# Graph network with mixture of experts: one packed word per visit for TensorE's block numbers, and another order of its waits

## The chip, the cores and the metric

The kernel runs on 1 core of one Trainium2 chip. The metric is the device time of one execution in microseconds (us); what is given is the median of several runs. Before the change it is 3036.38 us, the median of 3 runs.

## What is computed

x has 3125 nodes of 768 features; src and dst name 50000 edges, sorted by dst. Three graph attention layers with 12, 12 and 1 heads stand in a residual branch, then a mixture of 8 experts with 2 chosen per token stands in a second one:

```python
def _gat_layer(x, W, attn_l, attn_r, bias, src, dst, num_heads, head_dim, use_elu):
    z = (x @ W).reshape(N, num_heads, head_dim)
    el = jnp.sum(z * attn_l, axis=-1)
    er = jnp.sum(z * attn_r, axis=-1)
    e = jax.nn.leaky_relu(el[src] + er[dst], NEG_SLOPE)
    m = jax.ops.segment_max(e, dst, num_segments=N)
    ex = jnp.exp(e - m[dst])
    denom = jax.ops.segment_sum(ex, dst, num_segments=N)
    alpha = ex / denom[dst]
    msg = alpha[:, :, None] * z[src]
    out = jax.ops.segment_sum(msg, dst, num_segments=N)
    out = out + z + bias.reshape(1, num_heads, head_dim)
    if use_elu:
        out = jax.nn.elu(out)
...
x = x + _L0_gnn_ref(_layernorm(x), ...)          # three layers, use_elu in the first two
x = x + _L0_ffn_ref(_layernorm(x)[None], ...)[0] # softmax of the top 2 router logits, 8 experts, 192 wide, exact gelu
```

The change touches only how TensorE finds its way in the sums over the edges (`out` and `denom`) and in the term `er[dst]`.

## The kernel before

Nodes lie in NB = 25 blocks of 128, edges in ET = 391 tiles of 128. As the edges are sorted by dst, a tile meets one block or a few; a pair of tile and block that meet is a **visit**, and there are V = ET + NB - 1 = 415. b(k), the block of visit k, depends on the edges, so the kernel works it out on the chip at the start. VectorE's prologue (L1254 to L1263) writes it in several layouts: `b_k`; `b_of` (L1260, L1261), five numbers for each of NG = 83 groups of G = 5 visits, which TensorE reads; `b_g` (L1257 to L1259), the first block of a group and of the next, which ScalarE reads; `ends`, the last visit of each block. `turns` (written at L1756) is read by GpSimd in the expert part (L641).

Each layer has a node sweep (z = x @ W, stored to a table in HBM) and then an **edge sweep** over the 415 visits. NBUF = 4 groups are one trip of a loop, U = 20 visits; 20 trips are rolled, the 21st (3 groups) is written out. For a visit:

- GpSimd gathers 128 rows of z by src into a slot of 20 (L672). It waits for s_agg, the count of visits that TensorE has added up, so that the slot is free.
- VectorE builds ST_b, the one-hot matrix of a group from the edge's place in the block (L1445).
- TensorE multiplies ST_b with `erp`, the er values of block b in three bf16 parts: three small matmuls at L1022 (`er_of_edges`), whose address comes from b. The last one of a group raises s_er.
- VectorE forms the exponents (L1475, L1480; L1457 to L1469 in the third layer), ScalarE takes exp (L821, L822) and builds the one-hot S (L830, L834).
- VectorE weighs the rows: L1492 in the first two layers (raises s_msg), S_weighted at L1498 and S at L1494 in the third. Five or six visits of a trip (SPLIT) go another way: ScalarE copies a leading part (L781, L784, L785), VectorE the rest (L1509; L1512, L1513), which raises s_rest.
- TensorE adds the visit to its block in PSUM (`add_up`, L1028 to L1049): four passes of 384 or so columns at L1047 into banks that are chosen by the parity of b, then s_agg rises.
- Once a block is complete, ScalarE copies its sums out and clears the banks (`close_blocks`, L788; L805, L810, L814), which raises s_acc_free. It reads `b_g` at L790.

Each engine runs its own instruction list, and they meet in semaphores only. On TensorE `body` (L1051) sets the order: for each group g it loads the five block numbers of g (`now`), adds up visit 0, loads the five of g + ER_LEAD = g + 3 (`later`), and puts the er matmuls of group g + 3 behind the visits 1 (two of them) and 3 (three). Ahead of the loop the er matmuls of the groups 0 to 2 are done. A load (`blocks_of`, L1010 to L1015) is one instruction that fills five registers of TensorE's sequencer from SBUF. What depends on b is then computed by the sequencer: the address of `erp` (L1022), the value of the wait on s_acc_free (L1042), the bank (L1047). In `add_up` the waits come in this order: s_rest (L1035) or s_msg (L1039), s_acc_free (L1042), and s_S at the first visit of a group in the first two layers (L1044).

Of the kernel before, what the change touches and what calls it, by code (L numbers as in the profile page):

```python
# [8 lines left out]
I32 = mybir.dt.int32  # L9
U32 = mybir.dt.uint32  # L10
U8 = mybir.dt.uint8
# [14 lines left out]
G = 5  # L26
NBUF = 4
IN_ARENA = 3
ER_LEAD = 3
U = G * NBUF  # L30
VISITS = ET + NB - 1
V = -(-VISITS // G) * G
# [67 lines left out]
def gnn_ffn(nc, x, edges, gnn, ffn, out):  # L100
    with ExitStack() as ctx:
# [64 lines left out]
        src_k = sb("src_k", [P, V], I32)  # L166
        dst_k = sb("dst_k", [P, V])
        b_k = sb("b_k", [1, V + 1], I32)
        b_g = sb("b_g", [1, NG, 4], I32)
        b_of = sb("b_of", [1, NG + ER_LEAD, 8], I32)  # L170
        ends = sb("ends", [1, NB], I32)
        turns = sb("turns", [1, NS], I32)
        erm = sb("erm", [P, NB, 2 * HMAX])
        ert = sb("ert", [P, NB, HMAX])
        erp = sb("erp", [P, NB * 3 * 2 * HMAX], BF16)
# [753 lines left out]
        def _(pe):  # L929
# [74 lines left out]
            def edge_sweep(l):  # L1004
                H = HEADS[l]

                for bank in range(4):
                    nc.tensor.matmul(PS[:, bank, :], zeros_h[:, 0:P], zeros_h[:, :], start=True, stop=True)

                def blocks_of(g):  # L1010

                    return nc.values_load_multi_w_load_instructions(
                        b_of[0:1, bass.ds(g, 1), 0:G].rearrange("o i j -> o (i j)"), engines=[mybir.EngineType.PE],
                        min_val=0, max_val=NB - 1,
                        skip_runtime_bounds_check_because="b(k) is a sum of NB - 1 comparisons")[1]  # L1015

                def er_of_edges(g, jj, j, b):

                    if j == 0:
                        pe.wait_ge(s_ST, g + (NG * l + 1))  # L1020
                    for part in range(3):
                        o = nc.tensor.matmul(er_of(l, jj)[:, j, :], ST_b[:, jj, j * P:(j + 1) * P],  # L1022
                                             erp[:, bass.ds(b * (6 * H) + part * 2 * H, 2 * H)],
                                             start=(part == 0), stop=(part == 2))
                    if j == G - 1:
                        o.then_inc(s_er, 1)

                def add_up(g, i, jj, j, b):  # L1028

                    at = jj * G + j  # L1030
                    odd = (b + l) % 2
                    flat = PS[:, :, :].rearrange("p b n -> p (b n)")
                    if at in SPLIT[l]:
                        n = SPLIT[l].index(at)
                        pe.wait_ge(s_rest, len(SPLIT[l]) * i + (n + 1 + split_before(l)))  # L1035
                        onehot = S[:, jj, j, :]
                        rows = [parts[:, n, part, :] for part in range(2)]
                    else:
                        pe.wait_ge(s_msg, g * G + (V * l + j + 1))  # L1039
                        onehot = f32(S[:, jj, j, :]) if H > 1 else S_weighted[:, jj, j, :]  # L1040
                        rows = [edge_row(l, at)]
                    pe.wait_ge(s_acc_free, b + (NB * l + 1))  # L1042
                    if H > 1 and j == 0:
                        pe.wait_ge(s_S, g + (NG * l + 1))  # L1044
                    for c, n in ((0, HALF), (1, sum_width(l) - HALF)):
                        for row in rows:
                            o = nc.tensor.matmul(flat[:, bass.ds(odd * 1024 + 512 * c, n)], onehot,  # L1047
                                                 row[:, c * HALF:c * HALF + n], start=False, stop=True, skip_group_check=True)
                    o.then_inc(s_agg, 1)  # L1049

                def body(i, last):  # L1051
                    groups = LAST_GROUPS if last else NBUF
                    for jj in range(groups):
                        g = NBUF * i + jj
                        ahead = not last or jj + ER_LEAD < groups
                        now = blocks_of(g)
                        for j in range(G):
                            add_up(g, i, jj, j, now[j])
                            if j == 0 and ahead:
                                later = blocks_of(g + ER_LEAD)  # L1060
                            if j in (1, 3) and ahead:
                                for n in ((0, 1), (2, 3, 4))[j // 2]:
                                    er_of_edges(g + ER_LEAD, (jj + ER_LEAD) % NBUF, n, later[n])

                pe.wait_ge(s_erm, l + 1)
                for g in range(ER_LEAD):
                    now = blocks_of(g)
                    for j in range(G):
                        er_of_edges(g, g, j, now[j])
                with pe.Fori(0, NI - 1) as i:  # L1070
                    body(i, False)
                body(NI - 1, True)
# [126 lines left out]
        def _(dve):  # L1199
# [58 lines left out]
            link(nc.vector.tensor_copy(b_g[0:1, :, 0:1], starts[:, :, 0:1]))  # L1258
            link(nc.vector.tensor_copy(b_g[0:1, 0:NG - 1, 1:2], starts[:, 1:NG, 0:1]))  # L1259
            link(nc.vector.memset(b_of[0:1, :, :], 0))  # L1260
            link(nc.vector.tensor_copy(b_of[0:1, 0:NG, 0:G], starts))  # L1261
            link(nc.vector.tensor_copy(ends[0:1, 0:NB - 1], enter[0:1, :]))
            link(nc.vector.memset(ends[0:1, NB - 1:NB], V))  # L1263
            augment_first((2, 3, 4))
# [595 lines left out]
```

## Time and profile before

| | |
|---|---|
| median of 3 runs | 3036.38 us (3032.83 to 3039.52) |
| span of the profiled execution | 3059.8 us |
| TensorE matmuls | 2691.3 us busy (88%), 14056 instructions |
| VectorE | 2096.8 us (69%), 3895 |
| ScalarE | 1244.9 us (41%), 2607 |
| GpSimd | 1506.0 us (49%), 1528 |
| HBM | 253 GB/s over the span |

The profiled execution's own time is read by its span; it lies 23.4 us over the median of the runs. Busy times of different engines overlap, so they don't add up to the span. "<- issue" names idle time of an engine in which it waited for nothing that the profile shows. The edge sweeps lie at 258 to 903, 1116 to 1762 and 1965 to 2610 us or so.

### The profile page before, as it was taken

What the parts mean: (1) busy time and instruction counts of PE and PEld (TensorE: products, weight loads), DVE (VectorE), ACT (ScalarE), POOL (GpSimd) and SP (SyncE); (2) the same over time, 40 slices, a digit from 0 to 9 for tenths busy, and PEclk for the clock granted to TensorE, in tenths of its full rate; (3) what the DMA queues carried; (4) which work ended last, traced back from release to release, by engine and by line L of the source; (5) the groups of instructions that cost most, each with busy time, mean ns of one, the idle gap of its engine ahead of it and who ended that gap; (6) DMA issues with size and microseconds to landing.
All of it is one profiled execution on the core that took longest, in us unless ns stands there. A gap on an engine that the chain in (4) does not pass through costs nothing.

```text
span 3059.8 us, 57119 instructions
## 1 busy us (share of the span) xinstructions
PE 2691.3 (88%) x14056; PEld 1838.6 (60%) x14060; DVE 2096.8 (69%) x3895; ACT 1244.9 (41%) x2607; POOL 1506.0 (49%) x1528
## 2 busy tenths in 40 slices
PE   3997999998989979898989999788898889759998
PEld 2884555555558855555555578555555555547776
DVE  6776888888887768888878877545555555673332
ACT  1224555555544435555555544223222223622211
POOL 1005666666631156666666412466666665114443
PEclk9998999999999979999999999899999999979999
DMA  6447888888867878888888767788888887967776
GB/s 210 169 148 251 289 286 291 291 290 290 289 219 205 210 228 292 289 287 290 291 287 288 250 191 216 218 281 285 279 282 281 282 282 258 397 217 145 145 146 118
DMA packets 199261, 762.09 MB, mean 249 GB/s; under 512 B 41889, under 2 KB 58033, under 8 KB 198542
## 3 DMA queue, kind: packets, MB, share of 16 engines
q0 software_dynamic: 127632, 604.14, 64.8%
q1 hardware_dynamic: 53790, 108.21, 11.6%
q10 hardware_dynamic: 17760, 48.79, 4.0%
q8 instruction: 36, 0.59, 0.1%
q14 instruction: 43, 0.35, 0.0%
HBM read 640.01 MB, written 133.45 MB: 253 GB/s over the span
## 4 chain that ended last, share of the span: by engine, by line
PE 50%; DVE 21%; issue 13%; ACT 4%; DMA 4%; another core or an unknown queue 3%; SPq 2%; POOL 1%; DVEq 1%; ACTq 1%; POOLq 0%
PE PS L1047 30%; DVE arena L1492 5%; PE PS L1176 5%; PE PS L978 4%; PE PS L1165 4%; PE PS L980 2%; DVE parts L1509 2%; PE PS L1022 2%; DMA arena<-table,src_k 2%; SPq L493 1%; DVE ST_b L1445 1%; DVE arena L1357 1%; DVE arena L1367 1%; DVE arena L1335 1%
## 5 line engine op out<-in xcount | busy, mean ns | idle before, releaser
L672 POOL DMA_INDIRECT arena<-table,src_k x945 | 959.9, 1016 | 500.8 <-issue 213.1
L1047 PE MATMUL PS<-arena,S 128*128 128x384 f32 (+1 forms) x1848 | 706.8, 514 | 57.8 <-issue 46.3
L1492 DVE TENSOR_TENSOR arena<-arena,PS 128x768 f32<-128x768 f32 x630 | 575.2, 946 | 0.9 <-ACT arena L822 0.9
L1047 PEld LDWEIGHTS PS<-arena,S 128*128 128x128 f32 x1848 | 335.5, 194 | 282.7 <-issue 156.8
L1047 PE MATMUL PS<-parts,S 128*128 128x384 f32 (+2 forms) x1332 | 340.4, 375 | 57.2 <-issue 51.0
L672 POOL DMA_INDIRECT W<-table,src_k x300 | 295.9, 986 | 160.5 <-PE PS L1047 71.2
L1047 PE MATMUL PS<-arena,S_weighted 128*128 128x384 f32 (+1 forms) x840 | 319.9, 516 | 33.4 <-issue 25.3
L1022 PEld LDWEIGHTS PS<-erp,ST_b 128*128 128x128 bf16 x3735 | 193.9, 97 | 249.9 <-issue 184.2
L618 POOL DMA_DIRECT2D table<-arena x75 | 41.6, 555 | 557.7 <-DVEq L1379 382.3
L1047 PEld LDWEIGHTS PS<-parts,S 128*128 128x128 f32 x1332 | 223.7, 192 | 106.0 <-issue 97.5
L830 ACT ACTIVATE apart<-iota_row,dst_k 128x128 f32<-128x128 f32 x830 | 261.7, 389 | 60.8 <-issue 44.1
L781 ACT ACTIVATE parts<-arena 128x780 fp32r<-128x780 f32 x168 | 142.0, 849 | 309.2 <-DVE arena L1492 136.7
L1022 PE MATMUL PS<-erp,ST_b 128*128 x3735 | 213.0, 172 | 54.0 <-issue 38.9
L1047 PE MATMUL PS<-W,S 128*128 128x396 f32 (+1 forms) x640 | 239.8, 502 | 14.6 <-issue 8.1
L1047 PEld LDWEIGHTS PS<-arena,S_weighted 128*128 128x128 f32 x840 | 154.3, 196 | 143.7 <-issue 79.4
L978 PE MATMUL PS<-W_lead,S 128*128 128x512 f32 x450 | 190.4, 423 | 9.8 <-DVE xT_rest L1383 7.9
L1509 DVE TENSOR_TENSOR parts<-arena,parts 128x780 fp32r<-128x780 f32 x168 | 162.0, 964 | 35.7 <-issue 24.4
L1492 DVE TENSOR_TENSOR W<-W,PS 128x768 f32<-128x768 f32 x200 | 182.4, 944 | 0.0
L978 PE MATMUL PS<-W_lead,xT_rest 128*128 128x512 f32 x450 | 179.2, 398 | 0.0
L978 PE MATMUL PS<-W_rest_r,S 128*128 128x512 f32 x450 | 178.7, 397 | 0.0
L1047 PEld LDWEIGHTS PS<-W,S 128*128 128x128 f32 x640 | 116.1, 190 | 91.3 <-issue 39.0
L1795 DVE TENSOR_SCALAR arena<-PS,gate_of 128x768 f32<-128x768 f32 x56 | 57.0, 1018 | 162.5 <-PE PS L1176 162.5
(293 smaller groups left out, 4354.1 us busy)
## 6 DMA issues: line engine op xcount, KB each, us to landing
arena<-mixed SPq DMA_DIRECT2D x63, 384.0 KB, 3.6
table<-arena POOLq DMA_DIRECT2D x50, 396.0 KB, 3.3
local_b<-local SPq DMA_DIRECT2D x123, 160.0 KB
mixed<-sums ACTq DMA_DIRECT2D x50, 384.0 KB
arena<-table SPq DMA_DIRECT2D x50, 384.0 KB, 4.6
arena<-table,src_k POOLq DMA_INDIRECT x945
table<-arena POOLq DMA_DIRECT2D x25, 384.5 KB, 4.6
out<-last_bias POOLq DMA_DIRECT2D x25, 384.0 KB, 6.4
```

Of the source, the lines that this page charges most:

```text
L672: nc.gpsimd.indirect_dma_start(edge_row(l, k % U)[:, 0:table_width(l)], None, table[l][:, :], bass.IndirectOffsetOnAxis(src_k[:, k:k + 1]. ...
L781: nc.scalar.activation(parts[:, n, 0, 0:D + H], row[:, 0:D + H], ACT.Copy).then_inc(s_leading, 1)
L830: o = nc.scalar.activation(apart[:, j, :], iota_row[:, :], ACT.Abs, scale=-1.0, bias=dst_k[:, bass.ds(g * G + j, 1)])
L978: nc.tensor.matmul(PS[:, 4 + 2 * b.q, :], rows[x_part], W_parts[W_part][:, 0:512], start=start, stop=stop)
L980: o = nc.tensor.matmul(PS[:, 5 + 2 * b.q, 0:z_width(l) - 512], rows[x_part], W_parts[W_part][:, 512:z_width(l)], start=start, stop=stop)
L1022: o = nc.tensor.matmul(er_of(l, jj)[:, j, :], ST_b[:, jj, j * P:(j + 1) * P], erp[:, bass.ds(b * (6 * H) + part * 2 * H, 2 * H)], start=(p ...
L1047: o = nc.tensor.matmul(flat[:, bass.ds(odd * 1024 + 512 * c, n)], onehot, row[:, c * HALF:c * HALF + n], start=False, stop=True, skip_grou ...
L1165: o = nc.tensor.matmul(to, token_xT(b.q)[:, k * P:(k + 1) * P], WiT[:, k, bass.ds(e * FF, FF)], start=(k == 0), stop=(k == KC - 1))
L1176: o = nc.tensor.matmul(PS[:, 4 + 2 * b.q + c, 0:HALF], hT(b.q)[0:rows, j * P:(j + 1) * P], flat[0:rows, bass.ds(e * (2 * D) + (2 * c + j) ...
L1492: nc.vector.tensor_tensor(z, z, a, ALU.mult).then_inc(s_msg, 1)
L1509: nc.vector.tensor_tensor(low[:, 0:D + H], row[:, 0:D + H], f32(high[:, 0:D + H]), ALU.subtract).then_inc(s_rest, 1)
L1795: nc.vector.tensor_scalar(zr(b.q, D).rearrange("p (c d) -> p c d", c=2), PS[:, 4 + 2 * b.q:6 + 2 * b.q, 0:HALF], gate_of[:, bass.ds(b.n, 1 ...
```

## The change

`b_of` keeps five words for each group, and a word now holds two numbers: b of the visit, plus 256 times b of the visit three groups ahead (for the last three groups only the former). VectorE adds the second part in the prologue with one scalar_tensor_tensor. TensorE loads the words of a group once, takes `word & 255` where it used `now` and `word >> 8` where it used `later`; the second load of a group is gone. In `add_up` the waits are reordered: s_acc_free, then s_S, then s_rest or s_msg. `b_g` and `turns` are held in bytes.

```diff
@@ -27,6 +27,7 @@
 NBUF = 4
 IN_ARENA = 3
 ER_LEAD = 3
+LOW = 256
 U = G * NBUF
 VISITS = ET + NB - 1
 V = -(-VISITS // G) * G
@@ -166,10 +167,10 @@
         src_k = sb("src_k", [P, V], I32)
         dst_k = sb("dst_k", [P, V])
         b_k = sb("b_k", [1, V + 1], I32)
-        b_g = sb("b_g", [1, NG, 4], I32)
-        b_of = sb("b_of", [1, NG + ER_LEAD, 8], I32)
+        b_g = sb("b_g", [1, NG, 4], U8)
+        b_of = sb("b_of", [1, NG, 8], I32)
         ends = sb("ends", [1, NB], I32)
-        turns = sb("turns", [1, NS], I32)
+        turns = sb("turns", [1, NS], U8)
         erm = sb("erm", [P, NB, 2 * HMAX])
         ert = sb("ert", [P, NB, HMAX])
         erp = sb("erp", [P, NB * 3 * 2 * HMAX], BF16)
@@ -1011,8 +1012,14 @@
 
                     return nc.values_load_multi_w_load_instructions(
                         b_of[0:1, bass.ds(g, 1), 0:G].rearrange("o i j -> o (i j)"), engines=[mybir.EngineType.PE],
-                        min_val=0, max_val=NB - 1,
+                        min_val=0, max_val=(NB - 1) * (LOW + 1),
                         skip_runtime_bounds_check_because="b(k) is a sum of NB - 1 comparisons")[1]
+
+                def now(word):
+                    return (word & (LOW - 1)).with_bounds(min_val=0, max_val=NB - 1)
+
+                def later(word):
+                    return (word >> 8).with_bounds(min_val=0, max_val=NB - 1)
 
                 def er_of_edges(g, jj, j, b):
 
@@ -1030,6 +1037,9 @@
                     at = jj * G + j
                     odd = (b + l) % 2
                     flat = PS[:, :, :].rearrange("p b n -> p (b n)")
+                    pe.wait_ge(s_acc_free, b + (NB * l + 1))
+                    if H > 1 and j == 0:
+                        pe.wait_ge(s_S, g + (NG * l + 1))
                     if at in SPLIT[l]:
                         n = SPLIT[l].index(at)
                         pe.wait_ge(s_rest, len(SPLIT[l]) * i + (n + 1 + split_before(l)))
@@ -1039,9 +1049,6 @@
                         pe.wait_ge(s_msg, g * G + (V * l + j + 1))
                         onehot = f32(S[:, jj, j, :]) if H > 1 else S_weighted[:, jj, j, :]
                         rows = [edge_row(l, at)]
-                    pe.wait_ge(s_acc_free, b + (NB * l + 1))
-                    if H > 1 and j == 0:
-                        pe.wait_ge(s_S, g + (NG * l + 1))
                     for c, n in ((0, HALF), (1, sum_width(l) - HALF)):
                         for row in rows:
                             o = nc.tensor.matmul(flat[:, bass.ds(odd * 1024 + 512 * c, n)], onehot,
@@ -1053,20 +1060,18 @@
                     for jj in range(groups):
                         g = NBUF * i + jj
                         ahead = not last or jj + ER_LEAD < groups
-                        now = blocks_of(g)
+                        words = blocks_of(g)
                         for j in range(G):
-                            add_up(g, i, jj, j, now[j])
-                            if j == 0 and ahead:
-                                later = blocks_of(g + ER_LEAD)
+                            add_up(g, i, jj, j, now(words[j]))
                             if j in (1, 3) and ahead:
                                 for n in ((0, 1), (2, 3, 4))[j // 2]:
-                                    er_of_edges(g + ER_LEAD, (jj + ER_LEAD) % NBUF, n, later[n])
+                                    er_of_edges(g + ER_LEAD, (jj + ER_LEAD) % NBUF, n, later(words[n]))
 
                 pe.wait_ge(s_erm, l + 1)
                 for g in range(ER_LEAD):
-                    now = blocks_of(g)
+                    words = blocks_of(g)
                     for j in range(G):
-                        er_of_edges(g, g, j, now[j])
+                        er_of_edges(g, g, j, now(words[j]))
                 with pe.Fori(0, NI - 1) as i:
                     body(i, False)
                 body(NI - 1, True)
@@ -1258,7 +1263,10 @@
             link(nc.vector.tensor_copy(b_g[0:1, :, 0:1], starts[:, :, 0:1]))
             link(nc.vector.tensor_copy(b_g[0:1, 0:NG - 1, 1:2], starts[:, 1:NG, 0:1]))
             link(nc.vector.memset(b_of[0:1, :, :], 0))
-            link(nc.vector.tensor_copy(b_of[0:1, 0:NG, 0:G], starts))
+            link(nc.vector.tensor_copy(b_of[0:1, :, 0:G], starts))
+            blocks = bk_f()[0:1, :].rearrange("o (g j) -> o g j", j=G)
+            link(nc.vector.scalar_tensor_tensor(out=b_of[0:1, 0:NG - ER_LEAD, 0:G], in0=blocks[:, ER_LEAD:, :], scalar=float(LOW),
+                                                in1=blocks[:, 0:NG - ER_LEAD, :], op0=ALU.mult, op1=ALU.add))
             link(nc.vector.tensor_copy(ends[0:1, 0:NB - 1], enter[0:1, :]))
             link(nc.vector.memset(ends[0:1, NB - 1:NB], V))
             augment_first((2, 3, 4))
```

## Rows read from the trace of the kernel before

**Rows 1.** the page: its span, and the chain that ended last, by line

```profile
span 3059.8 us, 57119 instructions
...
PE PS L1047 30%; DVE arena L1492 5%; PE PS L1176 5%; PE PS L978 4%; PE PS L1165 4%; PE PS L980 2%; DVE parts L1509 2%; PE PS L1022 2%; DMA arena<-table,src_k 2%; SPq L493 1%; DVE ST_b L1445 1%; DVE arena L1357 1%; DVE arena L1367 1%; DVE arena L1335 1%
```

**Rows 2.** three windows: us, PE, PEld, DVE, ACT, POOL busy, PEclk, DMA share, GB/s

```profile
261.00:902.00 641.00, 582.72 (x2860) 348.47 (x2860) 534.86 (x768) 348.11 (x827) 411.06 (x406) 0.98 0.87 285
1118.00:1760.00 642.00, 574.56 (x2860) 345.11 (x2860) 534.91 (x769) 348.81 (x828) 407.83 (x405) 0.98 0.86 284
1967.00:2608.00 641.00, 570.42 (x2860) 348.98 (x2860) 344.79 (x1079) 183.89 (x404) 403.23 (x405) 0.97 0.86 278
```

**Rows 3.** TensorE's waits, whole run: us in total, times, longest

```profile
PE PS L1047 <- issue: 136.5, 283, 5.0
PE PS L1022 <- issue: 38.9, 70, 1.3
PE PS L952 <- DVEq L1269: 19.1, 1, 19.1
...
PE PS L1047 <- DVE arena L1492: 15.0, 19, 3.2
...
PE PS L1047 <- DVE S_weighted L1498: 6.9, 6, 5.7
...
PE PS L1047 <- ACT PS L814: 0.4, 2, 0.2
```

**Rows 4.** TensorE's sequencer, four lines: ns min/median/max, first and last start

```profile
L1012 PEldq TENSOR_LOAD <-b_of x498: 5/582/1751, 249.9 to 2596.9; - x166
L1012 PEldq FUSED_REGOPS  x360: 4/60/726, 261.5 to 2582.9; - x180
...
L1022 PEldq FUSED_REGOPS  x3735: 2/46/728, 250.8 to 2588.8; - x197
...
L1047 PEldq FUSED_REGOPS  x2490: 2/51/1412, 261.2 to 2602.2; - x192
...
L1042 PEldq ALU_OP  x1245: 2/32/737, 260.9 to 2601.5; - x178
```

**Rows 5.** the same columns, within 829.0 to 831.5 us alone

```profile
L1022 PEldq FUSED_REGOPS  x9: 46/46/46, 829.1 to 830.1; - x9
...
L1039 PEldq ALU_OP  x1: 32/32/32, 830.2 to 830.2; - x1
...
L1042 PEldq ALU_OP  x1: 32/32/32, 830.3 to 830.3; - x1
...
L1047 PEldq FUSED_REGOPS  x2: 46/70/93, 830.4 to 830.6; - x2
...
L1012 PEldq TENSOR_LOAD <-b_of x1: 581/581/581, 830.8 to 830.8; - x1
...
L1039 PEldq FUSED_REGOPS  x1: 42/42/42, 831.5 to 831.5; - x1
```

**Rows 6.** TensorE's timeline, two places: start us, us, ... [idle before <-releaser]

```profile
742.49 1.48 PE L1047 MATMUL PS<-arena,S 128*128 128x384 f32 x4
743.81 0.38 PE L1022 MATMUL PS<-erp,ST_b 128*128 x9
...
822.22 1.57 PE L1047 MATMUL PS<-W,S 128*128 128x384 f32 x4 [0.17 <-issue]
...
826.07 1.57 PE L1047 MATMUL PS<-arena,S 128*128 128x384 f32 x4 [0.54 <-issue]
```

**Rows 7.** L1012 within 824.0 to 826.1 us

```profile
L1012 PEldq TENSOR_LOAD <-b_of x1: 1404/1404/1404, 824.2 to 824.2; - x1
```

**Rows 8.** GpSimd's waits in the first edge sweep, 258 to 903 us

```profile
POOL arena L672 <- PE PS L1047: 69.5, 70, 2.3
```

**Rows 9.** the tiles b_of and b_g

```profile
L1261 DVE COPY b_of<-b_k x1: 580/580/580, 25.5 to 25.5; 1x415 int32<-1x415 int32 x1
...
L790 ACTq TENSOR_LOAD <-b_g x249: 4/494/907, 272.9 to 2601.3; - x125
```

## The prediction

> **What bounds the kernel now.** Start with the page: L1047, the line where TensorE adds the messages up, is alone 30% of the chain that ended last, in a span of 3059.8 us [rows 1]. It runs in the three edge sweeps, and there the change works.
>
> Next, the sweeps by themselves [rows 2]. They are equally long, 641 to 642 us, with 2860 matmuls each, though VectorE works 535 us in the first two and 345 us in the third, and ScalarE 348, 349 and 184 us. So neither sets the length. TensorE, busy 570 to 583 us at a clock of 0.97 to 0.98, comes nearest; it is idle 58 + 67 + 71 = 196 us in the three together, and that is all that a change of TensorE's orders alone can win.
>
> Then what ended this idle time [rows 3]: 136.5 us before L1047 and 38.9 us before L1022 end with "issue", 175 us of the 196. Late messages (L1492) end 15.0 us in 19 waits, late S_weighted 6.9 us in 6, the accumulator (L814) 0.4 us in 2. So TensorE waits for its own sequencer much more than for data.
>
> The sequencer's own instructions [rows 4]: 498 loads of block numbers (median 582 ns), 360 fused register operations for their addresses, a fused one for each er matmul (3735), two for each add_up (2490), and a plain ALU_OP for each wait on the accumulator (1245). What one of them holds up is read from starts, not durations [rows 5]: nine fused ones of L1022 start within 829.1 to 830.1, 0.125 us apart, with the order of their matmul between them; the ALU_OPs of L1039 and L1042 start at 830.2 and 830.3 and the next instruction at 830.4, so 0.1 us each though the rows say 32 ns; the load starts at 830.8 and the next one at 831.5, 0.65 us. A visit of er_of_edges costs the sequencer 3 x 0.125 = 0.375 us.
>
> **The sequencer's bill.** Removed: the second load in each group of the loop, 80 groups x 3 layers = 240 loads x 0.65 = 156 us, and half of the 360 address operations, 180 x 0.1 = 18 us. Together -174 us.
>
> Added: a word is no longer a block number. Each add_up takes word & 255 (1245), as do the er visits ahead of the loop (15 x 3 = 45); each er visit in the loop takes word >> 8 (240 x 5 = 1200). Together 2490 operations of a kind that the trace of before doesn't show. Nearest row: a plain ALU_OP such as L1042's, 0.1 us of the queue, +249 us. From below: the operation goes into a fused instruction that is there already; the two at L1047 last 46 and 93 ns [rows 5], so one more piece inside costs 0.047 us, +117 us; lower still, nothing. From above: each of the three er matmuls computes its own address (3735 at L1022), and if the shift is evaluated anew each time there are 3600 in place of 1200, +240 us more. I take 0.1 us, once per visit, since L1042 shows an operation by itself as a plain instruction. The net is +249 - 174 = **+75 us** of sequencer time; the other ends are 117 - 174 = -57, -174, and 75 + 240 = +315.
>
> **How much of it reaches the array?** Four passes of an add_up take 1.32 us of the array (742.49 to the er matmuls at 743.81), the sequencer orders them in some 0.4 us (830.4 to 830.8, [rows 5]): there it gets ahead. Nine er matmuls take 0.38 us, and the sequencer needs 9 x 0.125 = 1.1 us for them: there it falls behind. Both show [rows 6]: 0.17 us of idle time at 822.22, and 0.54 us at 826.07, right after a load that held the sequencer from 824.2 for 1404 ns [rows 7]. The shifts stand in the er stretches, where the lead is used up, 5 x 0.1 us in a group; the ANDs stand at the add_ups, where cover is 1.3 us of passes; the removed load stood behind the first add_up of a group, under its passes. All of the +75 exposed is the upper end, none of it the lower. I take 0.4 of it, because half of what is added (the shifts) has poor cover and the rest good: **+30 us**. This is chosen between ends, not read.
>
> [...] The array went idle at 826.07 behind a load, though the passes before it had been ordered. [...]
>
> **The order of the waits.** add_up now waits for the accumulator, then S, then the message. While a message is late, the ALU_OP of L1042 (0.1 us), and its wait, are done beforehand instead of behind it. The late ones with a row are 19 + 6 [rows 3]; others arrive just ahead of their matmul and are hidden in "issue". At 0.1 us each it is -2.5 us for 25 and -12 for a tenth of the 1245 visits; nothing if passes cover it. I take **-8 us**. A cost where the accumulator is late: queued behind it are the message wait, which blocks nothing else on TensorE, and the next passes; it is late twice for 0.4 us in all [rows 3], so nothing, up to +1 us.
>
> **The small ones.** VectorE's prologue gets one operation over 400 words; the copy beside it takes 0.58 us [rows 9] and lies on the path, since TensorE waits 19.1 us at L952 for this prologue [rows 3]: +0.6 us, the smaller memset gives nothing to speak of. b_g and turns become bytes: the same number of loads, for b_g 249 of 494 ns on ScalarE [rows 9], and ScalarE isn't the bound; nothing, or 1 us either way. No DMA is added, removed or moved past another queue.
>
> **The sum.** +30 - 8 + 0.6 = +22.6 us on the profiled execution. Its span, 3059.8 us, is 23.4 us over the median of the runs, 3036.38; the difference is carried over: 3036.4 + 22 = **3058 us**.
>
> What is late next? GpSimd waits for a slot that an add_up frees 69.5 us in 70 waits of the first sweep [rows 8]: the gathers follow TensorE, so a slower TensorE delays them too and nothing makes it good; a faster one meets a DMA share of 0.86 to 0.87 [rows 2] before it gets 196 us back.
>
> **Rivals.**
> 1. *More of the bill is paid* (0.15). All of the +75 shows: 3036 + 75 - 8 = 3103; with the shift evaluated for each matmul 0.4 x 315 = 126, 3154. About 3090 is likeliest here. For it: a fused operation for each of three parts at L1022. Against: passes of 1.3 us over orders of 0.4 us.
> 2. *Faster* (0.30). Place: the load behind the first add_up of a group. One piece of 0.65 us, 1.4 us at times, empties the queue (0.54 us idle at 826.07), while scattered pieces of 0.1 us hide under passes. It decides once an operation holds the queue for less than 174 / 2490 = 0.07 us, or the load is exposed more than 249 / 174 = 1.4 times as much as the operations. With fused operations and an exposure of 0.4, 0.4 x -57 - 8 = -31: 3005. With half of the loads worth 0.3 us and no operation exposed, -36 - 8: 2992. For it: rows 6 and 7. Against: L1042, and that half of the operations stand where the lead is gone.
> 3. *No difference* (0.15). Orders hide under passes both ways, or the gathers set the pace (DMA share 0.87): 3028 to 3042.
> 4. *The change doesn't do what it says*: both loads remain in the code that is built. Then +249 of queue at 0.4 are +100, 3128. Its sign would be the 498 loads; I count it inside the 0.15 of rival 1.
>
> **How the numbers follow.** The forecast, partly exposed and slower, has 0.40 and holds 3043 to 3080. With rival 1 slower has 0.55; no difference 0.15; faster 0.30. The bound is 0.2%, 6 us, about what a measurement of this kernel can tell from no change. 2990 to 3100 takes in rival 2's reckoned times and most of rival 1, and leaves under 2 in 10 outside. As cases of both signs hold much of the chance, the likeliest one's own range of 3043 to 3080 is the one to compare.
>
> **What would show it.** L1012 keeps 258 loads and 180 fused ones. New ALU_OPs stand at the lines of now and later, some 2490; if instead the fused ones at L1047 and L1022 last longer, it is rival 2; with some 4900, rival 1. "Issue" before L1022 rises from 38.9 us by 20 or more, that before L1047 stays; waits on L1492 shrink; the three sweeps stay alike at 648 to 652 us. If they are shorter although the ALU_OPs are there, the exposure is what I had wrong.

## The result and the profile after

The changed kernel takes 3042.44 us (median of 20 runs, 3038.39 to 3049.03), the kernel before 3036.26 us (20 runs, 3030.68 to 3050.54): ratio 1.0022, with a 95% interval of 1.0014 to 1.003. It is 6.2 us slower. The forecast was 3058 us, 22 us slower.

The page of the changed kernel, its span and the chain by line:

```profile
span 3045.3 us, 58032 instructions
...
PE PS L1054 23%; DVE arena L1500 8%; PE PS L979 7%; PE PS L1181 5%; PE PS L981 4%; PE PS L1170 4%; DVE parts L1517 3%; DVE W L1500 2%; DMA arena<-table,src_k 2%; DVE ST_b L1453 2%; POOL arena L673 2%; SPq L494 2%; PE PS L1029 1%; PE PS L1154 1%
```

L1054 is the old L1047. The profiled execution is 14.5 us *shorter* than the one of before, though the medians say the reverse: single executions of either kernel differ by 10 to 20 us, so a difference of 6 us isn't read from two of them. What can be read is what kind of instruction stands where.

The changed kernel's own three sweeps, from the first er matmul to the last add_up, with the columns of [rows 2]:

```profile
252.00:894.00 642.00, 581.72 (x2904) 351.49 (x2903) 541.27 (x778) 347.71 (x830) 421.86 (x412) 0.98 0.88 289
1100.00:1743.00 643.00, 578.62 (x2905) 350.12 (x2905) 543.80 (x779) 347.77 (x829) 416.57 (x413) 0.98 0.87 288
1940.00:2586.00 646.00, 570.53 (x2905) 348.47 (x2905) 347.79 (x1089) 184.44 (x405) 412.25 (x415) 0.97 0.86 281
```

The sweeps of before, taken the same way, last 651, 651 and 653 us with TensorE busy 589, 580 and 576 us. So in this execution each sweep is 7 to 9 us shorter, at a clock of 0.97 to 0.98 (0.96 to 0.97 there) and nearly the same DMA share; the 648 to 652 us that the prediction named as a sign don't show in it. TensorE's waits (us in total, times, longest):

```profile
PE PS L1054 <- issue: 145.5, 215, 5.1
PE PS L1029 <- issue: 27.9, 49, 1.2
...
PE PS L1054 <- DVE parts L1517: 5.7, 6, 2.5
PE PS L1054 <- DVE arena L1500: 5.5, 11, 2.4
PE PS L1054 <- DVE S L1502: 4.7, 4, 3.5
...
PE PS L1054 <- DVE S_weighted L1506: 2.8, 8, 0.4
```

"Issue" before the old L1047 went from 136.5 to 145.5 us, that before the old L1022 from 38.9 to 27.9 [rows 3]: 173 us in both sorts, 175 before. Late messages fell from 15.0 to 5.5 us, while late parts rose from 3.4 (not among the rows of before) to 5.7 us and late S from 0.2 to 4.7.

TensorE's sequencer, where [rows 4] stood (ns min/median/max, first and last start):

```profile
L1013 PEldq TENSOR_LOAD <-b_of x258: 4/582/1428, 250.7 to 2575.7; - x129
L1013 PEldq FUSED_REGOPS  x180: 2/60/700, 274.0 to 2558.2; - x180
...
L1029 PEldq FUSED_REGOPS  x3735: 2/46/1396, 251.7 to 2567.3; - x197
...
L1029 PEldq ALU_OP  x45: 32/32/36, 251.6 to 1948.1; - x45
...
L1040 PEldq ALU_OP  x2490: 2/36/1393, 261.1 to 2580.1; - x192
...
L1054 PEldq FUSED_REGOPS  x2490: 2/51/1380, 262.5 to 2580.7; - x192
```

Here lies the first surprise. 258 loads and 180 address operations are left, as forecast. But of new plain operations there are 1245 (L1040 has 2490, an AND and the old addition for each visit) and 45 at L1029 ahead of the loop, not 2490: the shift left no instruction of its own. The second thing was there before as well, and I passed over it: the longest register operation lasts 700 ns and more, at every line, and the shortest 2 ns, where the median is 36 to 51 [rows 4]. The sequencer pauses now and then, and what follows a pause goes through in a rush. Three operations in a row, in the trace of before:

```profile
L1039 PEldq FUSED_REGOPS  x1: 700/700/700, 276.1 to 276.1; - x1
L1042 PEldq ALU_OP  x1: 701/701/701, 277.5 to 277.5; - x1
L1044 PEldq ALU_OP  x1: 701/701/701, 278.9 to 278.9; - x1
```

Each lasts 0.70 us, and they start 1.4 us apart, so that as much of the pause stands between the records as in them. The next three (L1047 twice, L1012) last 5, 4 and 10 ns and start within 0.05 us, at 280.3. Counted over the trace of before, 216 register operations of TensorE last over 400 ns, 177 of them 650 to 750, 146 us together; of after, 290, 200 us. Pauses between the records aren't in these sums.

### The profile page after: what moved, and what is told of

The parts are those of the page before. It is cut to its first block, busy times and chain, and to the rows that moved or that the text cites. A ratio compares the mean times of both kernels' runs of the same rounds, so it can differ in the third digit from the quotient of the medians.

```text
span 3045.3 us, 58032 instructions
## 1 busy us (share of the span) xinstructions
PE 2679.9 (88%) x14059; PEld 1834.6 (60%) x14060; DVE 2100.9 (69%) x3896; ACT 1242.8 (41%) x2607; POOL 1509.8 (50%) x1528
## 4 chain that ended last, share of the span: by engine, by line
PE 48%; DVE 23%; issue 14%; DMA 4%; another core or an unknown queue 3%; ACT 3%; POOL 2%; SPq 2%; DVEq 1%; ACTq 1%; POOLq 0%
PE PS L1054 23%; DVE arena L1500 8%; PE PS L979 7%; PE PS L1181 5%; PE PS L981 4%; PE PS L1170 4%; DVE parts L1517 3%; DVE W L1500 2%; DMA arena<-table,src_k 2%; DVE ST_b L1453 2%; POOL arena L673 2%; SPq L494 2%; PE PS L1029 1%; PE PS L1154 1%
## 5 line engine op out<-in xcount | busy, mean ns | idle before, releaser
L1054 PE MATMUL PS<-arena,S 128*128 128x384 f32 (+1 forms) x1848 | 699.4, 510 | 52.1 <-issue 43.9
L1054 PEld LDWEIGHTS PS<-arena,S 128*128 128x128 f32 x1848 | 335.4, 192 | 267.0 <-issue 122.9
L1054 PE MATMUL PS<-parts,S 128*128 128x384 f32 (+2 forms) x1332 | 336.5, 373 | 53.7 <-issue 47.1
L1054 PE MATMUL PS<-arena,S_weighted 128*128 128x384 f32 (+1 forms) x840 | 315.9, 512 | 38.1 <-issue 30.6
L1029 PEld LDWEIGHTS PS<-erp,ST_b 128*128 128x128 bf16 x3735 | 188.7, 97 | 239.7 <-issue 167.5
L1054 PEld LDWEIGHTS PS<-parts,S 128*128 128x128 f32 x1332 | 221.6, 190 | 98.6 <-issue 83.6
L1054 PE MATMUL PS<-W,S 128*128 128x396 f32 (+1 forms) x640 | 241.2, 508 | 18.5 <-issue 17.6
L1029 PE MATMUL PS<-erp,ST_b 128*128 x3735 | 210.2, 172 | 44.5 <-issue 27.9
L1054 PEld LDWEIGHTS PS<-arena,S_weighted 128*128 128x128 f32 x840 | 152.1, 194 | 149.5 <-issue 83.4
L1054 PEld LDWEIGHTS PS<-W,S 128*128 128x128 f32 x640 | 115.5, 191 | 98.8 <-issue 46.6
```

## The experiments

They ran in four sessions, four kernels each. The kernel before was run beside them each time, and it took 2821, 2806, 3065 and 3037 us. In the first two sessions no trace has a register operation over 400 ns; in the last two all have them (the kernel before itself left no trace in any of the four). The second and the last two sessions were on one chip. So the pauses come and go with the session, and on that chip the kernel before takes 230 to 260 us less without them. The whole difference lies in the edge sweeps: outside of them every trace, with pauses or without, takes 1103 to 1114 us, while the three sweeps together take 1932 us in the trace of the changed kernel above and 1698 us in after_again's. The two conditions are kept apart below as **without pauses** and **with pauses**; a time is compared with the kernel before of its own session only.

For each, the **bill** is what it adds to the start-to-start times of TensorE's sequencer over the kernel before, reckoned from medians or means of the rows. Theories and rivals with a letter are those of the texts on record before each run.

### First session, without pauses

**bytes_only.** The kernel before with three tiles in bytes.

```diff
-        b_g = sb("b_g", [1, NG, 4], I32)
-        b_of = sb("b_of", [1, NG + ER_LEAD, 8], I32)
+        b_g = sb("b_g", [1, NG, 4], U8)
+        b_of = sb("b_of", [1, NG + ER_LEAD, 8], U8)
...
-        turns = sb("turns", [1, NS], I32)
+        turns = sb("turns", [1, NS], U8)
```

> The kernel before, with b_of, b_g and turns held in bytes and nothing else. Theory A (the sequencer's instructions set the difference): within 2 us of before. Rival B (the byte layout itself costs, through another load duration at L1012 or L790): slower by 5 us or more, with a longer load in the sequencer's rows.

Measured 3022.09 against 2821.43 us, ratio 1.0709 (1.0684 to 1.0734). The row of its loads, and TensorE's wait:

```profile
L1012 PEldq TENSOR_LOAD <-b_of x498: 1216/1223/2609, 250.8 to 2555.6; - x166
```

```profile
PE PS L1047 <- issue: 99.7, 240, 1.8
```

A load of five bytes holds the sequencer 1.22 us, five 32-bit words 0.58 us [rows 4]. The changed kernel has b_g and turns in bytes but b_of in words, so this isn't in its bill. As a probe it was worth more than meant: 489 loads in the sweeps are each 0.64 us longer, a bill of +313 us, and the time rose by 201 us. It isn't bytes by themselves that are slow: ScalarE's load of two block numbers got no longer in bytes (473 ns in this run, 494 in words [rows 9]), nor GpSimd's of one value of turns (288 ns in the trace of before, 274 in bytes in after_again).

**order_only.** bytes_only with the waits in the new order.

```diff
+                    pe.wait_ge(s_acc_free, b + (NB * l + 1))
+                    if H > 1 and j == 0:
+                        pe.wait_ge(s_S, g + (NG * l + 1))
                     if at in SPLIT[l]:
...
                         rows = [edge_row(l, at)]
-                    pe.wait_ge(s_acc_free, b + (NB * l + 1))
-                    if H > 1 and j == 0:
-                        pe.wait_ge(s_S, g + (NG * l + 1))
```

> bytes_only with add_up's waits in the new order (accumulator, S, message). Theory A: faster than bytes_only by 3 to 10 us, as a plain instruction and its wait move ahead of the message. Rival C (the new order is what costs): slower than bytes_only by 5 us or more.

Measured 3021.96 us (ratio to before 1.0703, 1.0677 to 1.0729), 0.1 us from bytes_only. Neither the gain of theory A nor the cost of rival C is there.

**packed_only.** The changed kernel with the waits in the old order (the diff above, reversed).

> The changed kernel with the old order of the waits: one packed word, one load a group, word & 255 and word >> 8. Theory A (the 1245 ANDs at add_up are paid behind the message wait, the load was mostly covered): slower than before by 10 to 20 us, so slower than the changed kernel by 5 to 10. Rival C: as fast as before or faster, -5 to 0 us.

Measured 2818.53 us, ratio 0.9997 (0.9981 to 1.0013). Packed words cost nothing that shows. Theory A missed by 10 us or more.

**load_gone.** bytes_only, where er_of_edges takes the current block in place of the one three groups ahead.

```diff
-                            if j == 0 and ahead:
-                                later = blocks_of(g + ER_LEAD)
                             if j in (1, 3) and ahead:
                                 for n in ((0, 1), (2, 3, 4))[j // 2]:
-                                    er_of_edges(g + ER_LEAD, (jj + ER_LEAD) % NBUF, n, later[n])
+                                    er_of_edges(g + ER_LEAD, (jj + ER_LEAD) % NBUF, n, now[n])
```

> bytes_only without the second load of a group; er_of_edges takes the block of the visit now at hand in place of the one three groups ahead, so the er term is computed from other nodes' values. It prices the load alone. Theory A (load mostly covered): faster than bytes_only by 5 to 20 us. Rival D (the load is exposed by 0.3 us or more each): faster by 60 us or more. Rival E (the load is wholly covered): within 3 us.

Measured 2818.63 us, ratio 0.9999 (0.9985 to 1.0014). Against bytes_only it is 203 us faster: rival D's number, but the load that went was the long one of bytes. 240 loads x 1.28 us less and 21 us of addresses bring the bill from +313 to -16 us. Being 16 us of bill below the kernel before brings nothing that stands clear of the noise. The bill counts, and only above some level.

### Second session, without pauses

**after_again.** The changed kernel, unaltered.

> The changed kernel itself, beside the kernel before on the same chip. Theory A (sequencer pieces of some 700 ns, as in the first traces, make the sequencer the bound; where they are absent the change is covered): where the longest fused operation at L1029 lasts 0.1 us, the time is that of before within 3 us, some 2820; where it lasts 0.7 us or more, it is 3035 to 3045 and above before by 3 to 9 us. Rival F (the ANDs cost wherever they run): above before by 5 us or more in both cases.

Measured 2804.86 against 2806.43 us, ratio 0.9995 (0.9981 to 1.0008). Its sequencer:

```profile
L1013 PEldq TENSOR_LOAD <-b_of x258: 578/583/1952, 252.8 to 2344.3; - x129
...
L1029 PEldq FUSED_REGOPS  x3735: 46/46/97, 253.8 to 2333.3; - x197
...
L1040 PEldq ALU_OP  x2490: 32/36/36, 263.2 to 2348.2; - x192
```

The longest register operations of TensorE last 114 ns (at L1054), the shortest 32. TensorE's waits in it:

```profile
PE PS L1054 <- DVE parts L1517: 29.8, 42, 3.0
...
PE PS L1054 <- issue: 4.3, 14, 0.8
PE PS L1029 <- issue: 4.2, 7, 0.7
```

"Issue", 173 us with pauses, is 8.5 us; the array waits for parts instead. Two stretches of the same lines show what shift and AND cost (starts, in the last columns):

```profile
L1029 PEldq FUSED_REGOPS  x6: 46/46/88, 605.3 to 606.0; - x6
...
L1040 PEldq ALU_OP  x2: 36/36/36, 606.2 to 606.2; - x2
```

Of the three register operations of an er visit the first lasts 83 to 93 ns and the others 46: the shift sits inside the first one, once a visit, as a piece of some 40 ns. Over the run 3200 start-to-start times at L1029 average 142.8 ns (ten over 250 ns left out), against 127.5 in ten_words, which has no shift: 3600 x 0.0153 = 55 us. The two operations of L1040 start 0.1 us apart, the AND being one (median 0.097 us). So the bill of the change is 1290 x 0.097 + 55 - 240 x 0.641 - 180 x 0.118 = 125 + 55 - 154 - 21 = **+5 us**, not +75. The two operations of L1054, which choose the bank, last 74.3 ns on average against 72.2 in ten_words, another 5 us that this sum leaves out.

**second_load.** The changed kernel with the load put back.

```diff
                             add_up(g, i, jj, j, now(words[j]))
+                            if j == 0 and ahead:
+                                again = blocks_of(g)
                             if j in (1, 3) and ahead:
                                 for n in ((0, 1), (2, 3, 4))[j // 2]:
-                                    er_of_edges(g + ER_LEAD, (jj + ER_LEAD) % NBUF, n, later(words[n]))
+                                    er_of_edges(g + ER_LEAD, (jj + ER_LEAD) % NBUF, n, later(again[n]))
```

> The changed kernel with a second load of the same words behind the first add_up of a group, used for word >> 8; so the load alone is put back. Theory A: within 3 us of the changed kernel where the 700 ns pieces are absent; 10 to 40 us slower than it where they are there. Rival D (a load is exposed wherever it runs): 60 us or more slower in both.

Measured 2857.65 us, ratio 1.0191 (1.017 to 1.0212), 51 us over before at a bill of +159. TensorE's wait:

```profile
PE PS L1054 <- issue: 34.3, 110, 1.1
```

Theory A said 3 us and rival D 60: it is 53 us over the changed kernel, 0.2 us for each load. By the bill a load in that place would be free in the kernel before; no run takes it out of there by itself.

**all_fused.** Words of 16 bits, fields swapped, no AND and no other plain operation for them.

```diff
-        b_of = sb("b_of", [1, NG, 8], I32)
+        b_of = sb("b_of", [1, NG, 8], mybir.dt.uint16)
...
-                def now(word):
-                    return (word & (LOW - 1)).with_bounds(min_val=0, max_val=NB - 1)
+                def now(word):
+                    return (word >> 8).with_bounds(min_val=0, max_val=NB - 1)
...
-                def later(word):
-                    return (word >> 8).with_bounds(min_val=0, max_val=NB - 1)
+                def later(word):
+                    return (word - (word >> 8) * LOW).with_bounds(min_val=0, max_val=NB - 1)
```

The prologue writes 256 times the current block plus the later one accordingly.

> The changed kernel with the words in 16 bits and the two fields swapped, the current block as word >> 8 and the later one as word - (word >> 8) * 256, which the sequencer takes inside instructions that are there anyway: 1245 ANDs are gone. The load of 16-bit words may be longer (five bytes took 1.22 us, five 32-bit words 0.58). Theory A: equal to the changed kernel within 3 us where the 700 ns pieces are absent, if the load lasts under 0.7 us; with them 5 to 25 us faster. If the load lasts 1.2 us: slower by up to 10 us in the first case.

Measured 2841.39 us, ratio 1.013 (1.0109 to 1.0152), 35 us over before. The load and L1040:

```profile
L1013 PEldq TENSOR_LOAD <-b_of x258: 1217/1222/2665, 250.8 to 2375.2; - x129
...
L1040 PEldq FUSED_REGOPS  x1005: 62/69/77, 262.9 to 2379.3; - x168
L1040 PEldq ALU_OP  x240: 32/32/32, 271.8 to 2366.2; - x120
```

The load is the long one (expected up to +10 us; it is +35), and the fused operations are longer too: 69 ns for 32 at L1040, 166 ns from start to start at L1029. Bill: 249 x 0.639 + 1005 x 0.036 + 3600 x 0.0385 - 154 - 21 = 159 + 36 + 139 - 175 = +159 us.

**ten_words.** One load of ten plain words, AND kept, no shift. The prologue writes the later blocks as five words of their own.

```diff
-        b_of = sb("b_of", [1, NG, 8], I32)
+        b_of = sb("b_of", [1, NG, 16], I32)
...
-                        b_of[0:1, bass.ds(g, 1), 0:G].rearrange("o i j -> o (i j)"), engines=[mybir.EngineType.PE],
+                        b_of[0:1, bass.ds(g, 1), 0:2 * G].rearrange("o i j -> o (i j)"), engines=[mybir.EngineType.PE],
...
-                                    er_of_edges(g + ER_LEAD, (jj + ER_LEAD) % NBUF, n, later(words[n]))
+                                    er_of_edges(g + ER_LEAD, (jj + ER_LEAD) % NBUF, n, words[G + n])
```

> The changed kernel with ten plain words in one load in place of five packed ones; the AND stays, the shift goes. It prices the length of a load and the shift. Theory A: a load of ten words lasts 0.6 to 1.2 us; equal to the changed kernel within 5 us where the 700 ns pieces are absent. If the shift inside the fused operations of L1029 cost something, this would be faster.

Measured 2808.11 us, ratio 1.0014 (0.9999 to 1.0028). Its load and er operations:

```profile
L1013 PEldq TENSOR_LOAD <-b_of x258: 1070/1078/2367, 251.8 to 2340.4; - x129
...
L1029 PEldq FUSED_REGOPS  x3735: 46/46/52, 253.3 to 2330.0; - x197
```

Ten words take 1.08 us, five 0.58: 0.1 us a word. That is what an AND takes (0.097 us). A packed word that needs an AND is a load of one word traded for an operation of the same price; that is why the change balances. Bill: 125 - 154 - 21 + 249 x 0.496 = +73 us, and it costs 1.7 us.

Put in order of their bills, the runs without pauses lie on a line with a bend:

| kernel | bill, us | time over before, us |
|---|---|---|
| load_gone | -16 | -3 |
| packed_only, after_again | +5 | -3, -2 |
| ten_words | +73 | +2 |
| all_fused | +159 | +35 |
| second_load | +159 | +51 |
| bytes_only, order_only | +313 | +201, +201 |

The first three rows can't be told from no difference. Bill less cost is 124, 108 and 112 us in the last three. By these three, some 110 to 120 us of bill are free, and beyond that each microsecond costs about one. The bend is known to some tens of us only: all_fused and second_load have one bill and differ by 16 us, and a bill from medians leaves out loads that last over 0.3 us more than theirs. There are 7 of these in all_fused (7 us beyond the median together), 19 in second_load (15 us) and 46 in bytes_only (43 us).

### Third session, with pauses

**after_third.** The changed kernel.

> The changed kernel once more. Theory A' (the sequencer's bill is the sum of start-to-start times of its instructions; some 115 us of bill are free where there are no 700 ns pauses, beyond that each us costs one): the change adds +6 us of bill (125 for 1290 ANDs at 0.097, 56 for the shifts inside 3600 er operations at 0.0156, less 154 for loads and 21 for addresses). Without pauses: within 3 us of before. With pauses (before at about 3036): +6 us.

Measured 3075.75 against 3065.21 us, ratio 1.0037 (1.0023 to 1.0051).

**order_old.** packed_only again.

> The changed kernel with the old order of the waits. Theory A': within 3 us of the changed kernel without pauses; with pauses 0 to 5 us slower than it. Rival C (the new order costs the 6 us of the result): 5 us or more faster than the changed kernel, where pauses are there.

Measured 3072.68 us, ratio 1.0025 (1.0016 to 1.0034). It is 3 us faster than the changed kernel and their intervals overlap, so the new order gave no gain here either; it may have cost up to 3 of the 10.5 us, and rival C's 5 us are not reached. In the traces the new order has 39 more instructions on TensorE's queue, all of them waits (58029 instructions against 57990).

**and_alone.** The kernel before, with an AND that changes no value (and b_g and turns in bytes).

```diff
-                            add_up(g, i, jj, j, now[j])
+                            add_up(g, i, jj, j, (now[j] & 255).with_bounds(min_val=0, max_val=NB - 1))
```

> The kernel before, both loads and 32-bit words kept, with & 255 on the block of each add_up (which changes no value): +121 us of bill. Theory A': 0 to 12 us slower than before without pauses, about 120 slower with them. Rival F (an AND is exposed at each add_up wherever it runs): 60 us or more slower in both.

Measured 3078.59 us, ratio 1.0041 (1.0027 to 1.0054): 13 us for a bill of +121, a ninth of what theory A' said. Its span, with the number of instructions:

```profile
span 3080.4 us, 58364 instructions
```

**two_ands.** second_load with `(word & 8191) & (LOW - 1)`.

> The changed kernel with the second load put back and a second AND on each word of add_up: +285 us of bill over before. Theory A': 285 - 115 = 170 us slower than before without pauses, 285 with them. Rival G (the cost grows in proportion, as 51 for 160 did): 90 us.

Measured 3109.04 us, ratio 1.0146 (1.013 to 1.0161): 44 us for +285. A' fell. Its page and L1040:

```profile
span 3104.1 us, 59559 instructions
...
L1040 PEldq ALU_OP  x3735: 2/36/728, 263.4 to 2642.6; - x197
```

155 register operations over 400 ns are left (101 us), where after_third has 332 (223 us). More work in the sequencer, fewer pauses. What rose along with the time is the number of instructions: 57119 before [rows 1], 58029 in after_third (+910), 58364 in and_alone (+1245), 59559 here (+2440). The first two give 10.5 and 13.4 us, about 0.011 us an instruction. But both add plain register operations (1290 and 1245), so these two can't tell the number of all instructions from the number of this kind.

### Fourth session, with pauses

Bill and number had to be pulled apart.

**after_fourth.** The changed kernel.

> The changed kernel once more. With pauses (before at 3030 to 3070, rows of 700 ns at register operations): 5 to 11 us slower than before. Without them: within 3 us.

Measured 3046.45 against 3036.51 us, ratio 1.0028 (1.0019 to 1.0037).

**bytes_again.** bytes_only: bill +313, no instruction more.

> bytes_only again: +313 us of sequencer time over before, not one instruction more. Theory R (in the state with pauses the number of instructions that the sequencer issues sets the time, and pauses give way where the bill grows): with pauses within 20 us of before, and the pauses nearly gone. Theory A' (the bill is paid 1:1 on top of the pauses): 200 us or more slower than before. Without pauses both say some 200 us slower, as it was.

Measured 3070.26 us, ratio 1.0106 (1.0091 to 1.0121): +34 us. Page, loads and er operations:

```profile
span 3068.8 us, 57122 instructions
...
L1012 PEldq TENSOR_LOAD <-b_of x498: 17/1222/2762, 251.9 to 2604.8; - x166
...
L1022 PEldq FUSED_REGOPS  x3735: 2/46/1381, 253.4 to 2596.3; - x197
```

Pauses are down to 54 (36 us). 201 us without pauses became 34 with them; theory R's bound of 20 us was too low, A' is out by 166.

**fused_again.** all_fused: bill +159, some 380 instructions fewer than before.

> all_fused again: +158 us of bill over before, about 115 instructions more than before and 800 fewer than the changed kernel. Theory R: with pauses within 5 us of before, so faster than the changed kernel. Theory A': with pauses 30 us or more slower than before. Without pauses some 35 us slower than before, as it was.

Measured 3035.69 us, ratio 0.9993 (0.9984 to 1.0002). The page's count:

```profile
span 3034.8 us, 56742 instructions
```

I had put its number at 115 more than before, by a miscount; it is 1290 fewer than the changed kernel. It is 10.8 us faster than that, at a bill 154 us higher. Without pauses it was the other way round, by 36.5 us. It has 2295 plain operations fewer than the changed kernel and 1005 fused ones more. Against before it has 985 plain ones fewer, which at 0.01 us each would be 10 us, and 377 instructions fewer in all, which would be 4 us; it is 0.8 us faster, at most 5 by the interval. That speaks for the number of all instructions, unless the bill of +159 makes up the rest.

**act_extra.** The changed kernel, and ten increments per group, on ScalarE, of a semaphore that nothing waits for.

```diff
                         leading(g, i, jj)
+                        for _ in range(10):
+                            act.sem_inc(s_tick_act)
```

> The changed kernel with 2490 more semaphore increments of 17 ns on ScalarE's queue in the edge sweeps; TensorE's instructions are as they were. Rival S (the pauses come from something that TensorE and ScalarE share, so that any instruction costs): with pauses 10 us or more slower than the changed kernel. Theory R in its narrow form (TensorE's own instructions alone): within 5 us of it. Without pauses: within 5 us.

Measured 3054.55 us, ratio 1.0062 (1.0048 to 1.0075), 8.1 us slower than the changed kernel. The page and the new rows:

```profile
span 3052.8 us, 60522 instructions
...
L844 ACTq EVENT_SEMAPHORE  x2490: 3/17/711, 267.1 to 2584.3; - x192
```

ScalarE works 41% of the span, 2490 x 17 ns are 42 us of its queue. Its own long register operations rose from 43 to 185, TensorE's from 276 to 298. The expectations left 5 to 10 us undecided, so this favours rival S without settling it; an instruction of ScalarE costs 8.1 / 2490 = 0.003 us, one of TensorE three times that. It wasn't run without pauses, so that the 8 us belong to them is not shown.

## Why the prediction was off

**The direction was right, the size wasn't**: slower by 6.2 us of the 22 forecast. 3042.44 us lies within 2990 to 3100, but just below the 3043 to 3080 that the forecast called its own, and at the edge of rival 3's 3028 to 3042. And the direction was luck: with the bill as measured and the other terms as they stood, the sum is 0.4 x 5 - 8 + 0.6 = -5 us, faster.

- *What bounds the kernel.* "TensorE waits for its own sequencer much more than for data" held: 173 us of "issue" again. But I took the waits to be the price of the instructions. They are nearly all gone (8.5 us) in a session without pauses, with the very same instructions. The maxima of 726 to 1412 ns stood in [rows 4]. The load of 1404 ns in [rows 7] is something else: the operations before and after it last 32 to 60 ns, and loads of over 0.88 us come without pauses too (15 of 258 in after_again, the longest 1952 ns; 12 of 498 before). Why these are long no run shows.
- *"that is all that a change of TensorE's orders alone can win"*, 196 us of idle time. This was wrong as well: without pauses the sweeps of the changed kernel are 234 us shorter, and TensorE's busy time in them falls from 1731 to 1634 us; in bytes_only, where the sequencer is late without pauses, it is 1716 us. The same matmuls have longer records where the sequencer is late, so idle time understated what it costs.
- *"I take 0.1 us and once per visit, since L1042 shows an operation by itself as a plain instruction."* **This is the term that failed.** It held for the AND (0.097 us, 1290 of them); the 1200 shifts went into instructions that were there, 55 us in place of 120. The end from below, 0.047 us a piece, was nearest for them (some 0.045). With this the bill is +5, not +75: 65 less for the shifts, and 5 less for the rounding of the other prices. Of the signs named, the 258 loads and 180 address operations came; new plain operations were about half the 2490, and the fused ones at L1029 lasted longer, which was rival 2's sign. "Issue" before the er matmuls fell in place of rising by 20.
- *"+30 us", an exposure of 0.4.* An exposure as a share was the wrong shape. Without pauses it is 0 up to 110 or 120 us of bill and 1 beyond; with pauses 313 us of bill cost 34 us. In the result's own condition the count fits better: +910 instructions at 0.011 us, a price taken from the 10.5 us of after_third, would be 10 us, and 9.9 and 6.2 were measured besides. Of the 6.2 us the bill, at the exposure that bytes_again shows (34 / 313), explains half a microsecond. That the count of instructions makes up the rest is argued from fused_again and not shown: a price on plain operations alone isn't ruled out, and up to 3 us may come from the order of the waits.
- *"-8 us" for the order of the waits.* 0: order_only 0.1 us from bytes_only, packed_only and after_again alike against before, order_old 3 us on the other side, if anything. The 19 late messages became 11, and parts and S, which come by the same engine, were late in their place.
- *The small ones.* The bytes of b_g and turns and the prologue's operation can't be told from nothing: after_again is 1.6 us faster than before with both in it, well within the noise. The loads themselves took 473 ns in place of 494 (b_g) and 274 in place of 288 (turns).
- *Rivals.* Rival 3, orders hidden under passes, came nearest without pauses (after_again within 3 us of before, 8.5 us of "issue"), up to the 110 to 120 us of bill that the runs left free; the rival names no such end. With pauses 173 us of "issue" stand before the array. Rival 1's premise of three shifts a visit and rival 2's starving load didn't occur: by the bills, second_load pays 51 us because the ANDs had used the reserve up.

**Open:** what the pauses are. They depend on the session. They fall on the queues of TensorE and ScalarE: 216 and 68 register operations over 400 ns in the trace of before, 72 of the 2490 increments in act_extra's, and none of the 2701 register operations of the other engines before. And they get fewer where the sequencer has more to do: 54 in bytes_again beside 276 in after_fourth, 155 in two_ands beside 332 in after_third. What causes them was not shown. Nor is the price of an instruction one number: two_ands and bytes_again pay 17 to 34 us beyond their count. And the rate of instructions isn't one either: the traces with over 150 of these operations pass 20.4 (before) to 22.3 (act_extra) instructions of all engines in a microsecond of the sweeps.

No version beat both kernels in either condition. The nearest, all_fused, ties with before with pauses and loses 35 us without.

## What to carry to other kernels

Price an unpacked field against the word that it saves: here a loaded 32-bit word and a plain register operation both hold the sequencer 0.1 us, so only a field whose unpacking goes into an instruction that is there anyway can be a gain (1200 shifts took 55 us of the bill, the subtractions of all_fused 139). Read the minimum and maximum of register operations before summing medians; where 2 ns and 700 ns stood in one row here, the medians didn't give the time, and fewer instructions were worth more than shorter ones (fused_again, 1290 fewer, is 10.8 us faster at a bill 154 us higher). Without pauses the sequencer's bill had a reserve here, 110 to 120 us, and then cost about in full, so measure where the bend lies before multiplying by a share.

## What the runs showed that I had not expected

- Loading five bytes, or five 16-bit words, takes TensorE's sequencer 1.22 us, five 32-bit words 0.58 us, ten 1.08 us.
- A shift goes into a fused register operation (46 to between 83 and 93 ns), an AND with 255 does not (36 ns, 0.097 us from start to start).
- The same kernel on the same chip took 2806 us in one session and 3065 and 3037 us in later ones, and the changed kernel's traces beside it have 0, 332 and 276 register operations over 400 ns.
- 2490 increments on ScalarE's queue, which has time to spare, cost 8 us with pauses.
- A pause is 0.70 us in most records, and the longest loads of block numbers (1.4 us and more) come with pauses and without.
